# Ten small loads issued from ScalarE's queue, and the bias row's product made in front of the first projections

## What is computed

```python
def attn(x, ...):                         # x is layer-normalised, D = 256, R = 64
    Q = x @ WQ.T;  K = x @ WK.T;  invQ = Q @ Winv.T;  invK = K @ Winv.T
    counts = arange(1, T + 1)
    z = cumsum(x) / counts
    fwd = (Q @ V_b) * cumsum(K @ W_b)
    inv = cumsum(invK @ V_b) * (invQ @ W_b)
    tri = (Q @ V_t) * cumsum(K @ W_t) * (z @ X_t)
    out = (fwd @ U_b.T + counts * bias_b
           + alpha_bi * (inv @ U_b.T + counts * bias_b)
           + alpha_tri * (tri @ U_t.T + counts * bias_t)) / counts
    return out @ WO.T
x = x + attn(layernorm(x), ...)
```

## Time and profile before

| | |
|---|---|
| median of 3 runs | 540.25 us (540.16 to 540.3) |
| profiled execution | 540.15 us, span from first to last instruction 538.4 us |
| busy in the span | PE 521.7 us (97%), DVE 451.3 (84%), POOL 410.9 (76%), ACT 342.8 (64%) |
| chain of work that ended last | PE 72%, DVE 15%, issue 6%, ACT 4%, POOL 1% |
| DMA, share of the span by its slices | high in the first two of 40 slices (about 27 us), near zero from 75 us on |

### The profile page before, as it was taken

How to read it: one execution, slowest core, us unless ns; L and a number is a source line. 1 busy time by engine, 2 the same in 40 slices (tenths; PEclk the granted TensorE clock), 3 DMA queues, 4 the chain that set the end, 5 groups by cost and what they waited for, 6 DMA issues and landing times.

```text
span 538.4 us, 10582 instructions
## 1 busy us (share of the span) xinstructions
PE 521.7 (97%) x3084; PEld 454.9 (84%) x3084; DVE 451.3 (84%) x1118; ACT 342.8 (64%) x811; POOL 410.9 (76%) x639
## 2 busy tenths in 40 slices
PE   8898899999999999999999998999999999999996
PEld 5777788888888888888888886998899999999996
DVE  3798889777897867969589689998899999999886
ACT  3555844737437474563675767787788888888763
POOL 4267939859589497697787937889988888888854
PEclk9999999999999999999999999999999999999999
DMA  8720500000000000000000000000000000000001
GB/s 234 214 80 2 162 0 2 0 2 1 1 1 0 2 0 2 2 0 1 1 2 2 0 1 1 11 19 19 13 22 22 21 20 19 19 19 19 21 19 50
DMA packets 16130, 13.86 MB, mean 26 GB/s; under 512 B 3883, under 2 KB 15839, under 8 KB 16095
## 3 DMA queue, kind: packets, MB, share of 16 engines
q1 hardware_dynamic: 16095, 13.43, 8.0%
HBM read 9.23 MB, written 4.19 MB: 25 GB/s over the span
## 4 chain that ended last, share of the span: by engine, by line
PE 72%; DVE 15%; issue 6%; ACT 4%; POOL 1%; DVEq 0%; ACTq 0%; POOLq 0%
PE ps L1062 16%; PE ps L1064 15%; PE ps L1063 15%; PE ps L1265 10%; PE ps L1453 3%; PE ps L1253 2%; PE ps L1263 2%; DVE parts L1541 2%; PE ps L1184 1%; PE ps L1401 1%; DVE X L1606 1%; PE ps L1313 1%; DVE gz L1627 1%; DVE xn_sums L1571 1%; DVE st L1612 1%
## 5 line engine op out<-in xcount | busy, mean ns | idle before, releaser
L1062 PE MATMUL ps<-keys_h,nT_h 128*128 128x256 f32 (+6 forms) x272 | 85.8, 315 | 1.4 <-DVE keys_l L1541 1.0
L1063 PE MATMUL ps<-keys_l,nT_h 128*128 128x256 f32 (+6 forms) x272 | 83.1, 306 | 0.0
L1064 PE MATMUL ps<-keys_h,nT_l 128*128 128x256 f32 (+6 forms) x272 | 83.1, 305 | 0.0
L1062 PE MATMUL ps<-parts,xq_parts 128*128 128x512 f32 (+1 forms) x192 | 74.6, 388 | 0.0
L1064 PE MATMUL ps<-parts,xq_parts 128*128 128x512 f32 (+1 forms) x192 | 72.0, 375 | 0.0
L1063 PE MATMUL ps<-parts,xq_parts 128*128 128x512 f32 (+1 forms) x192 | 71.8, 374 | 0.0
L1265 PE MATMUL ps<-V,probT 128*128 128x256 f32 x288 | 67.4, 379 | 0.0
L774 ACT ACTIVATE prob<-ps,nbias 128x205 f32<-128x205 f32 (+7 forms) x32 | 25.7, 803 | 61.9 <-DVE nbias L1633 61.8
L1265 PEld LDWEIGHTS ps<-V,probT 128*128 128x128 f32 x288 | 54.6, 190 | 7.6
L1062 PEld LDWEIGHTS ps<-keys_h,nT_h 128*128 128x128 f32 x272 | 51.3, 189 | 5.8 <-DVE keys_l L1541 1.2
L1063 PEld LDWEIGHTS ps<-keys_l,nT_h 128*128 128x128 f32 x272 | 51.3, 189 | 3.2
(11 more groups left out here) (236 smaller groups left out, 1594.1 us busy)
## 6 DMA issues: line engine op xcount, KB each, us to landing
X<-in_x_dram SPq DMA_DIRECT2D x8, 512.0 KB, 4.6
out_dram<-X SPq DMA_DIRECT2D x32, 128.0 KB, 1.7
early<-in_L_ffn_w_down_dram SPq DMA_DIRECT2D x1, 704.0 KB, 6.9
early<-in_L_ffn_w_gate_dram SPq DMA_DIRECT2D x1, 640.0 KB, 4.5
early<-in_L_ffn_w_up_dram SPq DMA_DIRECT2D x1, 640.0 KB, 5.8
ctx_rows<-in_ctx_dram SPq DMA_DIRECT2D x1, 308.0 KB
early<-in_L_attn_Winv_dram SPq DMA_DIRECT2D x1, 256.0 KB, 3.8
early<-in_L_attn_WQ_dram SPq DMA_DIRECT2D x1, 256.0 KB, 3.6
```

Of the source, the lines that this page charges most:

```text
L1062: mm(o, wh, mh, start=start, stop=False, **kw)
L1063: mm(o, wh, ml, start=False, stop=False, **kw)
L1064: return mm(o, wl, mh, start=False, stop=stop, **kw)
```

## The change

Three things are done together. Ten of the loads (V_t, W_t, X_t, the two biases, the two alphas, and the norm column, norm row and gate row) leave SyncE's list and stand at the head of ScalarE's. TensorE's list gets `turn_weight(2, wo)` in front of `spread_inv_count`, and `make_bias_row` between that and the first projections, no longer behind them. To feed it, ScalarE copies `woT` ahead of the two `inv_row` copies, and VectorE makes the products of alphas and biases ahead of the low parts of the folded weights. The waits are renumbered for the new order.

```diff
@@ SyncE
-            load(1, (wq, rows(WQ)), (wk, rows(WK)), (rkq[:, :, 4 * R:5 * R], rows(V_t)), (rkq[:, :, R:2 * R], rows(W_t)),
-                 (xt[:], rows(X_t)))
+            load(1, (wq, rows(WQ)), (wk, rows(WK)))
             load_x(0, (1,))
             load(2, (wo, rows(WO)), (ub2[:, :, 0:R], rows(U_b)), (ut[:], rows(U_t)),
-                 (bb[:], bias_b.rearrange("(j p) -> p j", p=P)), (bt[:], bias_t.rearrange("(j p) -> p j", p=P)),
-                 (alphas[:, 0:1], alpha_bi.broadcast_to([P, 1])), (alphas[:, 1:2], alpha_tri.broadcast_to([P, 1])))
+                 )
             load(3, (qw, rows(q_w)), (kw, rows(k_w)), (gw, rows(gate_w)),
-                 (norm_col[:], norm_w.rearrange("(j p) -> p j", p=P)),
-                 (norm_row[:], norm_w.rearrange("(a n) -> a n", a=1).broadcast_to([P, D])),
-                 (gate_row[:], gate_b.rearrange("(a n) -> a n", a=1).broadcast_to([P, D])))
+                 )
@@ ScalarE
+            load(1, (rkq[:, :, 4 * R:5 * R], rows(V_t)), (rkq[:, :, R:2 * R], rows(W_t)), (xt[:], rows(X_t)))
+            load(2, (bb[:], bias_b.rearrange("(j p) -> p j", p=P)), (bt[:], bias_t.rearrange("(j p) -> p j", p=P)),
+                 (alphas[:, 0:1], alpha_bi.broadcast_to([P, 1])), (alphas[:, 1:2], alpha_tri.broadcast_to([P, 1])))
+            load(3, (norm_col[:], norm_w.rearrange("(j p) -> p j", p=P)),
+                 (norm_row[:], norm_w.rearrange("(a n) -> a n", a=1).broadcast_to([P, D])),
+                 (gate_row[:], gate_b.rearrange("(a n) -> a n", a=1).broadcast_to([P, D])))
             xn_half(0, 0, 0)
...
             xnT_half(0, 0)
+            act.wait_ge(prep_mm, 3)
+            a.activation(woT, ps[:, 2, :].rearrange("p (j n) -> p j n", j=KD), ACT.Copy).then_inc(prep_ev, 1)
             for h in range(2):
                 act.wait_ge(s_inv_spread, h + 1)
                 a.activation(inv_row[R:2 * R, h * HTOK:(h + 1) * HTOK], ps[R:2 * R, 4 + h, :], ACT.Copy).then_inc(s_inv_row, 1)
-            act.wait_ge(prep_mm, 3)
-            a.activation(woT, ps[:, 2, :].rearrange("p (j n) -> p j n", j=KD), ACT.Copy).then_inc(prep_ev, 1)
@@ TensorE
             turn_xn(0, 0, 0)
-            spread_inv_count()
             pe.wait_ge(w_in[2], 16 * 7)
             turn_weight(2, wo)
-            pe.wait_ge(prep_v, 2)
+            spread_inv_count()
+            make_bias_row()
+            pe.wait_ge(prep_v, 4)
             proj_tiles(0, (0, 1), (6, 7, 4, 5))
             pe.wait_ge(s_inv_row, 2)
             proj_tiles(0, (2, 3), (6, 7, 4, 5))
-            make_bias_row()
             make_out_w()
@@ VectorE
             norm1_half(0, 1, 1)
+            ve.wait_ge(w_in[2], 16 * 7)
+            v.tensor_scalar(ub2[:, :, R:2 * R], ut[:], alphas[:, 1:2], None, ALU.mult)
+
+            v.scalar_tensor_tensor(bb[:], bb[:], alphas[:, 0:1], bb[:], ALU.mult, ALU.add).then_inc(s_prep_chain, 1)
+            ve.wait_ge(s_prep_chain, 1)
+            v.scalar_tensor_tensor(bt[:], bt[:], alphas[:, 1:2], bb[:], ALU.mult, ALU.add).then_inc(prep_v, 2)
             ve.wait_ge(prep_ev, 1)
...
             xnT_low(0)
-            ve.wait_ge(w_in[2], 16 * 7)
-            v.tensor_scalar(ub2[:, :, R:2 * R], ut[:], alphas[:, 1:2], None, ALU.mult)
-
-            v.scalar_tensor_tensor(bb[:], bb[:], alphas[:, 0:1], bb[:], ALU.mult, ALU.add).then_inc(s_prep_chain, 1)
-            ve.wait_ge(s_prep_chain, 1)
-            v.scalar_tensor_tensor(bt[:], bt[:], alphas[:, 1:2], bb[:], ALU.mult, ALU.add).then_inc(prep_v, 2)
```

More of the change, by code:

```diff
@@ L917, in batch, with load @@
                             silu(0, 0, first=True)
+            def load(k, *pairs):
+                for dst, src in pairs:
+                    a.dma_start(dst, src, allow_slow_non_contiguous=len(src.shape) == 2 and src.shape[1] <= KD).then_inc(w_in[k], 16)
+            load(1, (rkq[:, :, 4 * R:5 * R], rows(V_t)), (rkq[:, :, R:2 * R], rows(W_t)), (xt[:], rows(X_t)))
[4 more added lines that the diff above has]
+                 (gate_row[:], gate_b.rearrange("(a n) -> a n", a=1).broadcast_to([P, D])))
             xn_half(0, 0, 0)
```

## The result

The changed kernel takes 543.93 us (median of 6 runs, 542.3 to 548.86) against 540.2 us (6 runs, 539.66 to 540.55): ratio 1.0081, interval 1.0041 to 1.0121, slower by 3.7 us. The forecast was 541.0 us, the range ended at 541.9 us. The profiled execution took 545.06 us, with a span of 543.3 us against 538.4.

The account below looks back on a forecast made before the run. The prologue's bound was projection tiles, VectorE's scan and four steps, `y_half(0, 0)`, then gapless TensorE to the scan at 34.35 us. -0.05 (front) + 0.75 (bias additions) = +0.7 on 540.15 profiled, given as 541.0 us; range 539.6 to 541.9.

Parts of the forecast that it names:

- The front of the projections: TensorE before the first projection: the idle hole from 15.49 to 16.32 us takes the 0.86 us bias product; -0.05 us.
- Behind the projections: TensorE after the projection tiles: 0.86 us less work, no gain; idle before `y_half(0, 0)` grows from 0.79 to about 1.7 us.
- the contacts: Before `y_half(0, 0)`: VectorE's two-operand steps L1585, L1591, L1593 blocked by GpSimd's additions; replay gives 0.75 us more.
- The bias additions: GpSimd's eight tiles start near 19.0 instead of 23.56 us and slow three VectorE steps; `y_half(0, 0)` +0.75 us.
- The loads: Kernel start: ten loads issued on ScalarE beside V_b's landing at 5.5 us, wanted at 7.40; booked zero.
- rival 2: Prologue: V_b past 7.40 us or normalised half past 12.4; each microsecond beyond costs one, 541.5 to 542 us; 12%.
- rival 4: TensorE's idle 1.7 to 2.6 us before `y_half`: clock falls to 1.2 GHz, some 2.6 us lost, 543.6 us; 5%.

Follow-up runs that it names:

- the order alone: Changed kernel's new compute order with all loads back on SyncE, against the kernel before: 541.97 us, ratio 1.003.
- the loads alone: Only the ten loads moved to ScalarE's queue, compute order of the kernel before, against that kernel: 541.3 us, ratio 1.0021.
- the gaps filled: Whole change plus products that only keep TensorE busy (20 not 12 at the start, ten ahead of `y_half`), against the kernel before: 544.12 us, ratio 1.0085.
- contacts taken away: New order, loads on SyncE, bias row copied before the second normalisation, GpSimd's second four additions waiting for `ranks`, against the kernel before: 539.6 us, ratio 0.9997.
- the filled gap: New order, all loads on SyncE, ten products keeping TensorE busy ahead of `y_half(0, 0)`, against the kernel before: 540.84 us, ratio 1.0017.
- the three loads: Only V_t, W_t and X_t at the head of ScalarE's queue, compute order of before, against the kernel before: 540.47 us, ratio 1.0.
- the control with one queue: Kernel before with V_t, W_t and X_t ahead of group 0 on SyncE's own queue, against the kernel before: 541.8 us, ratio 1.0023.
- the two kernels under "Which loads?": Whole change with the five 4-byte-element loads back on SyncE, or only those five on ScalarE, against the kernel before: 547.66 and 546.5 us.
- the element loads back: Whole change, but the five loads of 4-byte elements back on SyncE at their old places, against the kernel before: 547.66 us, ratio 1.0139.
- the two rows: Only the norm row and gate row at the head of ScalarE's queue, compute order of before, against the kernel before: 541.1 us, ratio 1.0009.

## Why the prediction was wrong

**The front of the projections: right, given the loads in time.** Then the bias product fills the hole: first projection at 16.21 us with no idle time, forecast 16.3 to 16.4.

**Behind the projections: right.** The 0.86 us that TensorE saves went into idle time, which grew from 0.79 to 2.56 us in the kernel with the order alone (0.86 saved, 0.80 for the contacts).

**The bias additions: right in mechanism and size.** +0.75 forecast, +0.80 at `y_half` with the order alone (26.25 - 25.45), +0.69 in the changed kernel. Taking the contacts away took the cost away.

**The loads: wrong, and this is the step that failed.** "I book zero". The prediction took the added bytes at 327 GB/s, 0.6 us against a room of 1.9 us, and let the alpha products "hide completely, if their loads are in". V_b landed 2.9 us later, and `make_inner` started 1.2 us later than before. The bound I gave, "some 1 us beyond the room", was nearly enough for V_b, and with the loads alone that was the loss, 1.1 us. The dearer half is group 2. Three things were left out.
- Group 2. The prediction let its loads keep the delay of U_t, 4.0 us, and land near 9.5 us; U_t, the last of them on SyncE, was issued at 6.8 us and not at 5.4, took 9.7 us and landed at 16.5 us. (Before, the last of the group landed at 12.6 us, its last issue being at 9.0 us.) The alpha products had been moved to a place where the cover is only as long as the loads are early. This alone is enough to put the first projection at 19.92 us, 3.6 us late, 0.8 us beyond what V_b and the half clock had cost by then. With the gaps filled it puts it at 19.21 us, 1.7 us beyond what V_b had cost.
- The issuing. I took ten issues at 0.51 us. From about 4.4 us on both issuers slowed down, and ScalarE's first activation came at 9.32 us and not 7.87. On ScalarE that still hid behind the other delays; on SyncE it is the 1.4 us by which U_t was issued later than I took it.

```profile
4.35 1.26 SPq L390 DMA_DIRECT2D early<-in_L_attn_WO_dram  x1
...
4.50 1.15 ACTq L918 DMA_DIRECT2D norm_col<-in_L_xattn_norm_w_dram  x1
```

- The two rivals together. A late load makes an idle gap, and an idle gap can let the clock fall. I had priced rival 2 (late load, 12%) and rival 4 (clock, 5%) as if one excluded the other, and rival 4 at one place only. Rival 2 was what happened, and in three of six runs the clock fell as well. What the falls added there is not shown; in the profiled run the one fall added nothing, being hidden behind group 2.

The Trainium skill's rule that I had quoted, DMA: Bandwidth & Descriptors, Issuing engines are not separate DMA queues, speaks of loads that interleave whichever engine issues them. The traces agree: in the changed kernel V_t landed at 4.7 us and not at 7.4, and V_b at 8.4 us and not at 5.5. The prediction set the rule beside its zero, and did not ask which load loses its place by it.

**The clock.** The chance of 5% was too low: with the order alone, with its gap of 2.56 us, it fell in five of ten runs; with gaps of 1.14 us (loads alone) and 1.23 us (contacts taken away) in none of ten each; and in the changed kernel it fell after 2.08 us and, in the same run, not after 2.38 us. The price was 1.8 us between the two groups of the order alone, and not 2.6.

## What to carry to other kernels

A queue is also an order of importance: by the landings here, loads moved to a second issuer no longer wait behind the urgent ones, but run beside them, and what was behind them now runs beside them as well. Ask of each load on the path by how much it can be late, and count what the change wants earlier (here group 2) together with what it makes later. Work that is pulled into an idle gap of one engine can start another engine's work earlier, into the arms of a third: look where the freed work meets steps that run slower beside it. And a gap that grows on TensorE is not free even off the path; in this kernel gaps of 1.9 to 2.6 us were followed by half the clock in some runs and not in others. Last, a list of starts along the path is no list of prices: a later wait can cover all that came before it, as the one for group 2 did here.

## What I had not expected of the hardware

A tie of some 0.01 us decides 0.6 us. Shifts of the prologue pass through the whole kernel one to one, but the traces of the two kernels differ by a further 0.6 us from one point on. In the kernel before, VectorE's sum L1647 (two SBUF operands) started just ahead of GpSimd's product:

```profile
120.41 0.42 DVE L1647 TENSOR_TENSOR X<-dmix,X 128x256 f32<-128x256 f32 x1
120.42 3.09 POOL L501 TENSOR_TENSOR V<-nrm,norm_row 128x256 f32<-128x256 f32 x4
```

In the changed kernel GpSimd was first by 0.02 us, and VectorE took 1.01 us:

```profile
124.73 3.00 POOL L497 TENSOR_TENSOR V<-nrm,norm_row 128x256 f32<-128x256 f32 x4
124.75 1.01 DVE L1653 TENSOR_TENSOR X<-dmix,X 128x256 f32<-128x256 f32 x1
```

From there on the distance between the traces is 4.9 us and not 4.3. The other traces bear it out. From the start of `y_half(0, 0)` to the end the span is 512.9 to 513.0 us in the seven in which VectorE was first at both places where the two meet so closely, and 513.6 to 513.7 us in the five in which GpSimd was first at one of them: at 120 to 125 us in the changed kernel, the filled gap and the three loads, at 192 us in the order alone and the control with one queue. (In the two kernels under "Which loads?" the clock fell within that stretch.) The margins are 0.08 us and less; twice both start in the same hundredth, once with each outcome. So 0.6 of the 4.9 us between the profiled runs is such a tie and not the change. That ties also make the spread of the kernel before (538.9 to 541.5 us over the sessions) fits its size, but was not tested.

The other is the slowed issuing: 0.47 us for an issue on SyncE before, 1.26 us for the first slow one in the changed kernel and 2.70 us for the same one, WO at 4.35 us, with the element loads back. In both kernels SyncE's issues before it took 0.45 to 0.50 us, although both engines were issuing. A second issuer is not needed for it: with all loads on SyncE, the kernel with the filled gap has one of 0.99 us, at 5.90 us. And with the two rows it is SyncE's fourth issue already, V_b's own at 2.30 us, that takes 1.58 us. What slows them is open.
